# Neighbour searches placed over the first three quarters of the attention stage

## The reference

```
x = x + relu(concat(ln(x), max over up to 25 neighbours of ln(x)) @ W + b)       # layer 0, graph part
x = x + sum over the 2 best of 8 experts, weight_e * (gelu(ln(x) @ W1_e + b1_e) @ W2_e + b2_e)
x = x + (8-head attention over ln(x), masked by the adjacency matrix) @ Wo + bo    # layer 1, graph part
x = x + sum over the 2 best of 6 experts, three matmuls with relu between
```

## Time and profile before

| | us |
|---|---|
| median of 3 timed runs | 3431.71 |
| lowest and highest | 3428.62, 3441.75 |
| profiled execution, first to last instruction | 3440.9 |
| TensorE busy, share of the span | 2589.0 (75%) |
| VectorE | 1840.7 (53%) |
| ScalarE | 1292.2 (38%) |
| GpSimd | 837.9 (24%) |

### The profile page before, as it was taken

The page is one execution under the profiler, slowest core; times in us unless marked ns, Lnnn a source line. Parts: engine busy times, 40 slices in busy tenths (PEclk is TensorE's granted clock), DMA queues, the critical chain, the costliest instruction groups (busy, mean ns, idle before and its releaser), DMA issues.

```text
span 3440.9 us, 48188 instructions
## 1 busy us (share of the span) xinstructions
PE 2589.0 (75%) x16137; PEld 1525.4 (44%) x16137; DVE 1840.7 (53%) x5404; ACT 1292.2 (38%) x1959; POOL 837.9 (24%) x917
## 2 busy tenths in 40 slices
PE   0018626997699878996799779995799789986697
PEld 0015423654365445554465445643465346543044
DVE  3224335843686357744685358734694379124903
ACT  1004212354334643264335433372335432452054
POOL 3533530433041502242042402252043400000000
PEclk9988867998899988998899889997899899997598
DMA  5523524422532433332542343242442241004100
GB/s 132 59 27 65 50 38 88 75 38 32 105 64 37 46 58 89 45 52 24 105 75 33 37 77 79 39 53 22 104 75 37 33 82 36 2 1 74 37 2 7
DMA packets 106030, 183.66 MB, mean 53 GB/s; under 512 B 19935, under 2 KB 56188, under 8 KB 105724
## 3 DMA queue, kind: packets, MB, share of 16 engines
q0 software_dynamic: 25344, 51.96, 17.5%
q1 hardware_dynamic: 80380, 128.07, 15.2%
HBM read 158.59 MB, written 20.97 MB: 52 GB/s over the span
## 4 chain that ended last, share of the span: by engine, by line
DVE 35%; PE 30%; issue 18%; DMA 7%; DVEq 5%; ACT 3%; SPq 1%; ACTq 0%
DVE parts L1034 15%; PE PH L1293 5%; PE PA L1339 5%; PE PY L1354 4%; PE PA L1342 4%; PE PY L1304 4%; DMA parts_dram<-parts 4%; DMA xn<-in_x 2%; DVE res_n L940 2%; ACT HB L1165 2%; DVE G L823 2%; DVEq L744 2%; DVE score L791 2%; DVE top L795 1%; DVE xn L773 1%
## 5 line engine op out<-in xcount | busy, mean ns | idle before, releaser
L716 POOL DMA_INDIRECT G<-table,slot_idx x792 | 811.4, 1024 | 372.8 <-issue 372.8
L1158 ACT ACTIVATE HB<-PH,bias_T 128x512 f32<-128x512 f32 x512 | 351.3, 687 | 862.4 <-PE PH L1293 862.4
L1034 DVE CUSTOM_DVE_ANT_0 parts<-PA,mask 128x1024 bf16<-128x1024 f32 x512 | 627.0, 1225 | 19.8 <-issue 19.8
L1165 ACT ACTIVATE HB<-PA 128x1024 f32<-128x1024 f32 x512 | 496.0, 1020 | 364.8 <-PE PA L1342 364.6
L1304 PEld LDWEIGHTS PY<-W_sb,HB 128*128 128x128 f32 x4096 | 512.3, 195 | 134.4 <-issue 87.9
L1304 PE MATMUL PY<-W_sb,HB 128*128 128x128 f32 x4096 | 521.3, 279 | 65.2 <-DVE res_n L940 53.7
L1293 PE MATMUL PH<-XT,W_sb 128*128 128x512 f32 x1024 | 527.0, 630 | 17.4 <-ACT HB L1158 17.4
L1316 PE MATMUL PA<-KS,QS 96*128 96x512 bf16 x1024 | 342.1, 420 | 114.2 <-DVE MX L1034 58.7
L1339 PE MATMUL PA<-QS,KS 99*128 99x512 bf16 x1024 | 393.6, 384 | 11.2 <-ACT HB L1165 7.4
L1342 PE MATMUL PA<-identb,mask 128*128 128x128 bf16 x4096 | 397.1, 218 | 0.0
L594 POOL TENSOR_TENSOR pool_pad<-pool_pad 1x1 f32<-1x1 f32 x112 | 23.6, 210 | 1520.4 <-DVE slot_idx L803 1275.0
(11 more groups left out here) (156 smaller groups left out, 2270.1 us busy)
## 6 DMA issues: line engine op xcount, KB each, us to landing
adj_sb<-in_adj SPq DMA_DIRECT2D x64, 512.0 KB, 4.2
adjm<-in_adj SPq DMA_DIRECT2D x64, 512.0 KB
G<-table,slot_idx POOLq DMA_INDIRECT x792
parts_dram<-parts SPq DMA_DIRECT2D x16, 768.0 KB, 6.9
QS<-parts_dram SPq DMA_DIRECT2D x48, 256.0 KB, 8.3
KS<-parts_dram SPq DMA_DIRECT2D x48, 256.0 KB, 8.1
xn<-in_x SPq DMA_DIRECT2D x8, 512.0 KB, 13.1
table<-xn SPq DMA_DIRECT2D x8, 512.0 KB, 3.5
```

What stands on the lines that cost most here:

```text
L716: pool.indirect_dma_start(G[:, t % 2, s, :], None, table, bass.IndirectOffsetOnAxis(slot_idx[:, t, s:s + 1], axis=0), bounds_check=ROWS - ...
L1034: ins = dve.tensor_tensor_reduce(out=junk, in0=psum(ps, step)[:, :], in1=mask[:, t, :], scale=1.0, scalar=LOWEST, op0=ALU.add, op1=ALU.max ...
L1158: act.activation(HB[:, i % 2, c, :], psum(ps, step)[:, :], ACT.Gelu, bias=bias_T[:, e * HC + c:e * HC + c + 1]).then_inc(*emptied(ps, step))
L1165: act.activation(HB[:, kc % 2, 2 * pr:2 * pr + 2, :], psum(ps, key)[:, :].rearrange("p (h q) -> p h q", h=2), ACT.Exp, scale=float(D) ** - ...
```

## The change

`spread` gets the first three quarters of the list, 68 * 3 // 4 = 51 steps, and the other 17 steps are appended with no search step between them. The 27 search steps are the same and in the same order. Nothing else of the kernel is changed. Passes without a search get the same list as before.

```diff
         s += second[1:2] + experts0(middle[1:])
-        s += spread(second[2:], finds[cut:])
+        body = second[2:]
+        most = len(body) * 3 // 4
+        s += spread(body[:most], finds[cut:]) + body[most:]
```

## The result

| | before | after |
|---|---|---|
| median, us (4 runs each) | 3434.57 | 3558.11 |
| lowest and highest | 3428.62, 3441.75 | 3546.64, 3563.49 |
| profiled execution, first to last instruction | 3440.9 | 3557.9 |

The change makes the kernel slower: the ratio is 1.0357, with a 95% interval from 1.0325 to 1.0389. The forecast was a span of 3557 us and a median of 3547 us. The changed code is two lines longer, so line L597 of before is L599 here, and so on.

What follows compares the result with a forecast made beforehand. It took GpSimd's gathers, then tile 6's maximum and fin (1,1), to set the attention stage's end. Its terms, 125.6 - 10.4 + 1 = +116 us, gave a span of 3557 and a median of 3547 us, range 3518 to 3578.

Steps and rivals of the forecast that it cites:

- part 1: Start of GpSimd's gathers: find 2 and max 0 can't move, so tile 6 lands when it did in passes 1 to 4; 0 us.
- part 3: Passes 5 and 6: indices of tile 3 and max 1 come earlier, so later tiles start 5.2 us sooner each; -10.4 us.
- part 2: VectorE's fin (1,0) falls behind max 6, with TensorE's rest of the last group behind it: +20.9 us a pass, 125.6 in six.
- part 5: TensorE's restart at half clock moves from the last expert unit to the last group: +0.3 us in passes 1 to 4, +1 us.
- part 4: Smaller moves (fin 01 later; degree counts, class products, adjacency loads earlier) are covered by TensorE's wait of some 31 us: 0 us.
- The first (gathers earlier): Gathers start earlier and TensorE's waits at fin (1,1) go, 94 us in all, so 3338 us; chance 4%.
- The second (the wait only changes its place): TensorE's wait moves from fin (1,1) to fin (1,0) and the stage ends as before: 3432 us; chance 4%.
- The fourth (half clock through the whole group): TensorE stays at half clock through the last group after its longer wait: up to 20.9 us a pass, 3672 us; chance 3%.
- The third (VectorE's load slows the gathers): With about 5 us less VectorE work beside them, gathers land tile 6 5 us earlier in six passes: 3517 us; chance 6%.

Runs made afterwards that it cites:

- the first two experiments: Max 5 moved behind fin (1,0) and max 6 to the end, against the changed kernel: 0.9964; only max 4 to 6 moved ahead of fin (1,0), against before: 1.0367.
- first experiment: Changed kernel with max 5 moved straight behind fin (1,0) and max 6 to the end of the attention part: 3421.14 us, ratio 0.9964 to the kernel before.
- second experiment: Kernel before with only max 4, 5 and 6 moved straight ahead of fin (1,0): 3559.01 us, ratio 1.0367.
- fifth, on the other chip: Changed kernel with find 2, its adjacency load and max 0 moved ahead of the second expert unit: 3510.47 us, ratio 1.0177 to the kernel before.
- sixth: Changed kernel with max 5 and 6 behind fin (1,0), and find 2 and max 0 ahead of the second expert unit: 3382.57 us, ratio 0.9811 to before.
- the cured one: Changed order with max 5 straight behind fin (1,0) and max 6 at the end: 0.9964; with early find 2 and max 0 as well: 0.9811.
- changed kernel with short gathers: Changed kernel with 4 transfers in place of 8 for tiles of the lowest class, four slots left out: 3366.52 us, ratio 0.9800 to the kernel before.

## Why the prediction was right

The forecast of a median of 3547 us is a ratio of 1.0336, inside the measured interval; the forecast span, 3557 us, is 0.9 us off. The mechanism is the one forecast. Some of the closeness is luck, as the terms show: the gathers' pace took off 6.9 us that no term had, and 6.6 us that no term had came on elsewhere. The terms come from the table of the six passes:

| term | forecast, us | measured, us |
|---|---|---|
| tile 6 lands, passes 1 to 4 (part 1) | 0 | -6.9 |
| tile 6 lands, passes 5 and 6 (part 3) | -10.4 | -11.3 |
| rest of the last group behind fin (1,0) (part 2) | +125.6 | +125.6, held by the first two experiments |
| restart, now in that group (part 5) | +1, with the next line | +14.0 |
| restart, no longer in the last expert unit (part 5) | in the line above | -11.1 |
| smaller moves (part 4) | 0 | 0 |
| outside the attention part | 0 | +6.6 |
| sum | +116 | +117 |

**Part 1, the start of the gathers: right.** Max 0 ends 22.5 us behind the origin in both kernels in passes 1 to 4. That tile 6 landed 2 us sooner in three of these passes is the pace of the gathers, not their start: from max 0 to the copy behind tile 6 it took 97.5 us before, and 95.5, 95.3, 97.3 and 95.2 us after.

**Part 2, fin (1,0) behind max 6: right.** Made alone it gives 1.0367; undone it gives 0.9964. The distance from fin (1,0) to fin (1,1) is 20.94 us of work, as read from the profile before, and 22.47 to 23.95 us as it runs now, a mean of 23.3; the 2.3 us on top belong to part 5. The prediction's count of what stands behind fin (1,0) is off by one, six score steps and not seven; the 20.94 us are read from the profile and do not hang on it.

**Part 3, passes 5 and 6: right.** The wait for indices went, find 3 starts 3.0 us earlier in the fifth pass (2.8 forecast), and fin (1,0) comes 5.1 and 6.1 us before the old fin (1,1) did; 5.2 each was forecast.

**Part 4, the smaller moves: right.** Fin (0,1) does come later, at 60.9 us behind the origin where it was 56.15, and TensorE's wait at fin (1,0) covers it: 29.87 us were measured in the second pass, 31 forecast.

**Part 5, the clock: right in size, its pieces a little too large.** The clock is at half speed for some 6 us after the wait, and the last group takes 2.3 us longer, a mean over six passes; 2.5 was forecast. The last expert unit gets 1.9 us back, where 2.2 was forecast, since it no longer follows a wait: in the second pass, from fin (1,1) to the add of proj(1) it was 9.63 us and is 7.74. The net is some +0.5 us a pass; the forecast was +0.3 in passes 1 to 4 and nothing in the last two.

**The rivals.** The first (gathers earlier) falls by max 0 at the same 22.5 us. The second (the wait only changes its place) falls by the 0.81 us that TensorE waits at fin (1,1), while the add of proj(1) comes 15.3 to 21.8 us later. The fourth (half clock through the whole group) falls by the granted clock of 1.00 over 16 us of it. The third (VectorE's load slows the gathers) had 6%. Tile 6 did land sooner in this run, by about 2 us, but nothing points to that cause. With fin (1,0) put back into the stretch of the gathers (first experiment) they took 95.3 to 96.0 us in passes 1 to 4, with find 5 put back (second) 94.8 to 95.3 us, and with both left out (fifth, on the other chip) 98.0 to 99.5 us. And the profile before is the slower one where the change touches nothing. GpSimd ready for tile 0 and for tile 7 of the second search, which runs without attention, before and after:

```profile
290.74 0.18 POOL L594 TENSOR_TENSOR pool_pad<-pool_pad 1x1 f32<-1x1 f32 x1 [68.17 <-DVE slot_idx L803]
...
469.83 0.18 POOL L594 TENSOR_TENSOR pool_pad<-pool_pad 1x1 f32<-1x1 f32 x1 [4.31 <-issue]
```

```profile
286.24 0.18 POOL L596 TENSOR_TENSOR pool_pad<-pool_pad 1x1 f32<-1x1 f32 x1 [66.81 <-DVE slot_idx L805]
...
462.81 0.18 POOL L596 TENSOR_TENSOR pool_pad<-pool_pad 1x1 f32<-1x1 f32 x1 [3.88 <-issue]
```

That is 179.1 us before and 176.6 after; the first two experiments have 176.1 and 175.8, the fifth and sixth 179.3 and 179.4. So the pace goes with the run: 1.4% less of 97.5 us is 1.4 of the 2 us, by this estimate. In the changed kernel's second pass, these are the stretches in which tiles 4 and 6 were fetched (busy time of PE, PEld, DVE, ACT, POOL; clock, DMA share, GB/s):

```profile
1162.40:1177.60 15.20, 13.81 (x132) 7.09 (x130) 5.82 (x14) 11.00 (x17) 8.37 (x11) 1.00 0.28 36
1193.80:1209.50 15.70, 0.00 (x0) 0.00 (x0) 1.59 (x5) 0.00 (x0) 8.32 (x11) 0.50 0.32 33
```

A tile took 15.2 us beside 5.82 us of VectorE work, and 15.7 us beside 1.59, with TensorE and ScalarE idle. So the pace does not follow VectorE's load. The Trainium skill, SBUF — State Buffer, section "SBUF: two separate sides", says that VectorE and GpSimd share a port pair under an exclusive lock; no run here shows it slowing these gathers.

## What to carry to other kernels

In a list of steps that every engine takes in order, a waiting step hands its wait to each step behind it, so ask of every waiting step what stands directly behind it, and how much of another engine's work hangs on that. Here the same 13 us wait for a gather cost some 21 us a pass more ahead of fin (1,0) than ahead of fin (1,1). And where the transfers run one behind the other at their own pace, an earlier place for the steps that consume them brings nothing; an earlier start of the first one does: with max 0 9.2 us sooner, the ratios give some 10 us a pass in the changed order (1.0357 to 1.0177) and some 9 in the cured one (0.9964 to 0.9811); the traces, with the slower gathers of the second chip, give 5 to 8 us in the changed order.

## What the runs showed of the hardware

- A tile's indirect gathers cost a share beside that of each transfer, and the share does not follow their number. From one tile's start to the next it took 30.9 us for 16 transfers, some 16 for 8, and 9.1 to 10.3 for 4 (second pass, changed kernel with short gathers). In the same passes, from the first transfer to the end of the last it took 21.6 us for 16, 10.1 to 10.9 for 8 and 4.9 to 6.1 for 4, so 1.2 to 1.5 us a transfer; the rest is 9.3, 5.0 to 6.0 and 4.2 to 4.5 us a tile. What that rest is made of, no run tells.
- The pace of the gathers varies by some 4% between runs of kernels that issue the same transfers (from max 0 to the copy behind tile 6, means of passes 1 to 4 from 95.1 us in the second experiment to 98.5 in the fifth, on the other chip), and the kernel before had medians of 3432.5 and 3450.5 us on two chips. The runs don't show why.
- A restart after some 30 us of standing still cost the last group about as much (2.3 us, a mean of the passes) as one after 12.28 us had cost the last expert unit (1.9 us).
